# Routing over 1024 tokens at a time, with the router as stationary operand in four column tiles

## What is computed

```python
x = x + 0.5 * ffn(layernorm(x))
x = x + attn(layernorm(x))
x = x + 0.5 * ffn(layernorm(x))

def ffn(x):                       # T = 8192 tokens, E = 32 experts, C = 320
    logits = xt @ w_router        # 512 x 32
    probs = softmax(logits);  top1 = argmax(probs);  gate = probs[top1]
    pos = cumsum(onehot(top1), axis=0)[t, top1] - 1
    accepted = pos < C
    slot = where(accepted, top1 * C + pos, E * C)
    buf[slot] = xt                # gather by expert
    y = (silu(buf @ w_gate) * (buf @ w_up)) @ w_down
    return xt + where(accepted, y[slot] * gate, 0)
```

## Time and profile before

| | us |
|---|---|
| median of 3 runs | 4491.49 (4490.32 to 4492.13) |
| profiled execution, time | 4491.09 |
| profiled execution, span | 4489.0 |
| r1, from the trace | 0 to 218 |
| r2, from the trace | 3414 to 3732 |
| PE busy over the span | 4281.2 (95%) |
| DVE busy over the span | 3158.3 (70%) |

### The profile page before, as it was taken

The page is one execution under the profiler, slowest core; times in us unless marked ns, Lnnn a source line. Parts: engine busy times, 40 slices in busy tenths (PEclk is TensorE's granted clock), DMA queues, the critical chain, the costliest instruction groups (busy, mean ns, idle before and its releaser), DMA issues. The chain is left out here.

```text
span 4489.0 us, 70758 instructions
## 1 busy us (share of the span) xinstructions
PE 4281.2 (95%) x24512; PEld 3068.9 (68%) x24512; DVE 3158.3 (70%) x5967; ACT 2154.7 (48%) x3603; POOL 2726.9 (61%) x1628
## 2 busy tenths in 40 slices
PE   7799999989999989999999999999996997999999
PEld 7789999968888744444444444444444886999998
DVE  7767777756666567777777777777763886777776
ACT  5543333322222136666666666666662443333332
POOL 2333444425555559999999999999992223443343
PEclk9999999989999979999999999999997997999999
DMA  5455555535555534444444444444424765555553
GB/s 181 134 205 187 181 186 187 187 132 176 175 178 178 160 86 96 96 96 96 96 98 99 99 99 99 96 96 97 98 66 166 243 209 183 188 187 183 181 178 117
DMA packets 473572, 650.63 MB, mean 145 GB/s; under 512 B 214300, under 2 KB 216624, under 8 KB 473248
## 3 DMA queue, kind: packets, MB, share of 16 engines
q1 hardware_dynamic: 440480, 579.32, 44.3%
q0 software_dynamic: 30720, 66.62, 3.9%
q10 hardware_dynamic: 2048, 0.53, 0.1%
HBM read 468.75 MB, written 194.58 MB: 148 GB/s over the span
## 5 line engine op out<-in xcount | busy, mean ns | idle before, releaser
L1628 DVE TENSOR_REDUCE att_halves<-att_mx 128x1 f32<-128x512 f32 x2048 | 1274.0, 683 | 487.2 <-PE att_mx L1677 487.1
L1561 ACT ACTIVATE att_p<-att_st 128x512 f32<-128x512 f32 x2048 | 1107.8, 598 | 419.9 <-PE att_st L1693 370.5
L1513 POOL TENSOR_TENSOR att_pairsum<-att_p,att_p 128x1024 f32<-128x1024 f32 x512 | 1209.4, 2386 | 143.3 <-ACT att_p L1561 140.2
L1693 PE MATMUL att_st<-att_q,att_k 128*128 128x512 f32 x2048 | 870.2, 427 | 9.2 <-ACT att_p L1561 4.4
L1677 PE MATMUL att_mx<-att_k,att_q 96*128 96x512 f32 x2048 | 822.1, 406 | 27.0 <-POOL att_q L1502 27.0
L1693 PEld LDWEIGHTS att_st<-att_q,att_k 128*128 128x128 f32 x2048 | 386.2, 189 | 541.0 <-ACT att_p L1561 277.4
L1703 PE MATMUL att_op<-att_p,att_v 128*32 128x512 f32 x4096 | 553.2, 601 | 0.7 <-ACT att_p L1561 0.7
L800 DVE TENSOR_TENSOR e_w<-e_raw,e_w 128x2048 fp32r<-128x2048 f32 x192 | 438.9, 2286 | 42.2 <-ACT e_w L795 42.2
L1677 PEld LDWEIGHTS att_mx<-att_k,att_q 96*128 96x128 f32 x2048 | 394.3, 193 | 108.4 <-issue 27.8
L819 ACT ACTIVATE e_sg<-e_gp 128x320 f32<-128x320 f32 x256 | 112.1, 438 | 731.3 <-PE e_up L182 731.3
L795 ACT ACTIVATE e_w<-e_raw 128x2048 fp32r<-128x2048 f32 x192 | 367.1, 1912 | 42.9 <-DMA e_raw<-in_w_gate 37.6
(11 more groups left out here) (153 smaller groups left out, 8318.5 us busy)
## 6 DMA issues: line engine op xcount, KB each, us to landing
e_raw<-in_w_gate SPq DMA_DIRECT2D x64, 1024.0 KB, 8.7
e_raw<-in_w_up SPq DMA_DIRECT2D x64, 1024.0 KB, 11.0
e_raw<-in_w_down SPq DMA_DIRECT2D x64, 1024.0 KB
att_q<-q SPq DMA_DIRECT2D x192, 256.0 KB, 4.1
att_k<-k SPq DMA_DIRECT2D x192, 256.0 KB, 6.3
r_ao<-ao SPq DMA_DIRECT2D x32, 1024.0 KB, 10.0
r_x<-in_x SPq DMA_DIRECT2D x16, 1024.0 KB, 8.2
x<-r_base SPq DMA_DIRECT2D x16, 1024.0 KB, 5.5
```

The costliest lines, as they stand in the source:

```text
L1513: nc.gpsimd.tensor_tensor(out=pairsum[h][PLACE[g]][:, :], in0=pr[h][2 * g % RING][:, :], in1=pr[h][(2 * g + 1) % RING][:, :], op=ALU.add). ...
L1561: nc.scalar.activation(pr[h][kt % RING][:, half(c)], st[(4 * kt + x) % NB][:, :], ACT.Exp, scale=SCALE).then_inc(s_exp, 1)
L1628: nc.vector.tensor_reduce(out=halves[:, h, qt, c:c + 1], in_=mx[n % NB][:, :], axis=AX.X, op=ALU.max).then_inc(s_max, 1)
L1693: nc.tensor.matmul(st[(4 * kt + x) % NB][:, :], kst[b][:, h, kt * P:(kt + 1) * P], qst[b][:, h, c * HALF:(c + 1) * HALF], start=True, stop ...
```

## The change

- One pass of choice, gates, positions and slots serves two groups, 1024 tokens in 8 tiles (`TR`), with w = r // 2. The tiles of the small quantities are twice as wide.
- `products(r)` now takes a whole group. The router's 128 x 32 slice is the stationary operand, put in column tile j for token tile j, and 128 tokens are streamed: 16 matmuls of 128 columns. The result is transposed, 4 x 32 experts in partitions, and lands in a `tp` tile. ACT copies it (`copy_turned`), and PE turns it back to tokens in partitions (`back`, one transpose of 128 x 128). `xnT` has 2 x 4 buffers, one for each tile of two groups.
- `positions(w)`: one triangular matmul over all 256 columns; for each of the tiles 0 to 6 one matmul of ones with its one-hot repeated over all later tiles (224 to 32 columns); one of ones with the running count repeated 8 times. 9 matmuls instead of 28 per 1024 tokens.
- POOL scatters 8 tiles behind each pass. x has 6 buffers in r1 and 5 in r2.
- The orders of ACT, DVE and PE are written anew, as the diff shows.

```diff
+TR = 2 * TJ
+NR = NG // 2
...
-    NX = 4
+    NX = 5 if attn else 6
...
-        xnT = S.pair(sb, "xnT", [P, KD, P])
+        xnT = [[sb(f"xnT{b}_{j}", [P, KD, P]) for j in range(TJ)] for b in range(2)]
+        turned = S.pair(sb, "turned", [P, P])
...
             def copies(r, js):
                 for j in js:
-                    n = TJ * r + j
-                    act.wait_ge(s_tp, n + 1)
-                    act.wait_ge(s_logits, past(n - 1))
-                    nc.scalar.activation(xnT[j % 2][:, :, :], tp[j % 2][:, :, :], ACT.Copy).then_inc(s_xnT, 1)
-
-            def exps(r):
-                act.wait_ge(s_shifted, r + 1)
-                act.wait_ge(pick.sem, pick.steps * r)
+                    u = (TJ + 1) * r + j
+                    act.wait_ge(s_tp, u + 1)
+                    act.wait_ge(s_logits, past(r - 1))
+                    nc.scalar.activation(xnT[r % 2][j][:, :, :], tp[u % 2][:, :, :], ACT.Copy).then_inc(s_xnT, 1)
+
+            def copy_turned(r):
+                u = (TJ + 1) * r + TJ
+                act.wait_ge(s_tp, u + 1)
+                act.wait_ge(s_logits, past(r - 1))
+                nc.scalar.activation(turned[r % 2][:, :], tp[u % 2][:, 0, :], ACT.Copy).then_inc(s_xnT, 1)
+
+            def exps(w):
+                act.wait_ge(s_shifted, w + 1)
+                act.wait_ge(pick.sem, pick.steps * w)
                 nc.scalar.activation(ex[:, :, :], shifted[:, :, :], ACT.Exp).then_inc(s_exp, 1)
 
...
             norm(0)
             norm(1)
             copies(0, range(TJ))
-            bases(0, range(TJ))
-            for r in range(NG):
-                exps(r)
-                if r + 1 < NG:
-                    copies(r + 1, (0, 1))
-                    bases(r + 1, (0, 1))
-                if r + 2 < NG and not attn:
-                    norm(r + 2)
-                if r + 1 < NG:
-                    copies(r + 1, (2, 3))
-                    bases(r + 1, (2, 3))
-                if r + 2 < NG and attn:
-                    norm(r + 2)
+            if attn:
+                bases(0, range(TJ))
+                for r in range(NG):
+                    copy_turned(r)
+                    if r + 1 < NG:
+                        copies(r + 1, (0, 1))
+                        bases(r + 1, (0, 1))
+                    if r % 2 == 1:
+                        exps(r // 2)
+                    if r + 1 < NG:
+                        copies(r + 1, (2, 3))
+                        bases(r + 1, (2, 3))
+                    if r + 2 < NG:
+                        norm(r + 2)
+            else:
+                norm(2)
+                copy_turned(0)
+                bases(0, range(TJ))
+                copies(1, range(TJ))
+                copy_turned(1)
+                bases(1, range(TJ))
+                for w in range(NR):
+                    r = 2 * w + 2
+                    if r < NG:
+                        copies(r, range(TJ))
+                    exps(w)
+                    if r < NG:
+                        copy_turned(r)
+                        norm(r + 1)
+                        bases(r, range(TJ))
+                        copies(r + 1, range(TJ))
+                        copy_turned(r + 1)
+                    if r + 2 < NG:
+                        norm(r + 2)
+                    if r < NG:
+                        bases(r + 1, range(TJ))
 
...
-            for r in range(NG):
-                if attn and r + 1 < NG:
-                    normalise(r + 1)
-                choose(r)
-                if attn:
-                    gates(r)
-                    if r + 2 < NG:
-                        bias(r + 2)
-                        measure(r + 2, (0, 1))
-                    slots(r)
-                    if r + 2 < NG:
-                        measure(r + 2, (2, 3))
-                else:
-                    if r + 2 < NG:
-                        measure(r + 2, (0, 1))
-                    gates(r)
-                    if r + 2 < NG:
-                        measure(r + 2, (2, 3))
-                    slots(r)
-                    if r + 2 < NG:
-                        normalise(r + 2)
+            if attn:
+                for r in range(NG):
+                    w = r // 2
+                    if r + 1 < NG:
+                        normalise(r + 1)
+                    if r % 2 == 0:
+                        if r + 2 < NG:
+                            bias(r + 2)
+                            measure(r + 2, (0, 1))
+                        if r + 3 < NG:
+                            bias(r + 3)
+                        if r + 2 < NG:
+                            measure(r + 2, (2, 3))
+                    else:
+                        if r + 2 < NG:
+                            measure(r + 2, (0,))
+                        choose(w)
+                        if r + 2 < NG:
+                            measure(r + 2, (1,))
+                        gates(w)
+                        if r + 2 < NG:
+                            measure(r + 2, (2,))
+                        slots(w)
+                        if r + 2 < NG:
+                            measure(r + 2, (3,))
+            else:
+                measure(2, range(TJ))
+                normalise(2)
+                for w in range(NR):
+                    r = 2 * w + 3
+                    choose(w)
+                    if r < NG:
+                        measure(r, range(TJ))
+                    gates(w)
+                    if r < NG:
+                        normalise(r)
+                    if r + 1 < NG:
+                        measure(r + 1, range(TJ))
+                    slots(w)
+                    if r + 1 < NG:
+                        normalise(r + 1)
 
...
             def turn(r, j):
-                n = TJ * r + j
-                pe.wait_ge(s_xn, n + 1)
-                pe.wait_ge(s_xnT, past(n - 1))
+                u = (TJ + 1) * r + j
+                pe.wait_ge(s_xn, TJ * r + j + 1)
+                pe.wait_ge(s_xnT, past(u - 1))
                 for k in range(KD):
-                    last = nc.tensor.transpose(tp[j % 2][:, k, :], xn[r % 2][:, j, k * P:(k + 1) * P], ident[:, :])
+                    last = nc.tensor.transpose(tp[u % 2][:, k, :], xn[r % 2][:, j, k * P:(k + 1) * P], ident[:, :])
                 last.then_inc(s_tp, 1)
 
-            def products(r, j):
-                pe.wait_ge(s_xnT, TJ * r + j + 1)
-                pe.wait_ge(s_shifted, r)
-                pe.wait_ge(s_top, 2 * TJ * r)
+            def products(r):
+
+                u = (TJ + 1) * r + TJ
+                pe.wait_ge(s_xnT, u)
                 for k in range(KD):
-                    last = nc.tensor.matmul(logits[:, j, :], xnT[j % 2][:, k, :], wr_sb[:, k, :],
-                                            start=k == 0, stop=k == KD - 1)
-                last.then_inc(s_logits, 1)
-
-            def positions(r):
+                    for j in range(TJ):
+                        last = nc.tensor.matmul(tp[u % 2][j * E:(j + 1) * E, 0, :], wr_sb[:, k, :], xnT[r % 2][j][:, k, :],
+                                                start=k == 0, stop=k == KD - 1)
+                last.then_inc(s_tp, 1)
+
+            def back(r):
+                w, par = r // 2, r % 2
+                pe.wait_ge(s_xnT, (TJ + 1) * (r + 1))
+                pe.wait_ge(s_shifted, w)
+                pe.wait_ge(s_top, 2 * TR * w)
+                nc.tensor.transpose(logits[:, par * TJ:(par + 1) * TJ, :].rearrange("p j e -> p (j e)"),
+                                    turned[par][:, :], ident[:, :]).then_inc(s_logits, 1)
+
+            def positions(w):
 
                 pe.wait_ge(s_setup, 1)
-                pe.wait_ge(s_onehot, r + 1)
-                pe.wait_ge(s_run, r)
-                pe.wait_ge(s_slots, r)
-                for j in range(TJ):
-                    nc.tensor.matmul(posp[:, j, :], tri[:, :], onehot[:, j, :], start=True, stop=False)
-                    for before in range(j):
-                        nc.tensor.matmul(posp[:, j, :], ones[:, :], onehot[:, before, :], start=False, stop=False)
-                    last = nc.tensor.matmul(posp[:, j, :], ones[:, :], run[:, :], start=False, stop=True)
-                last.then_inc(s_pos, 1)
+                pe.wait_ge(s_onehot, w + 1)
+                pe.wait_ge(s_run, w)
+                pe.wait_ge(s_slots, w)
+                nc.tensor.matmul(posp[:, :, :], tri[:, :], onehot[:, :, :], start=True, stop=False)
+                for j in range(TR - 1):
+                    nc.tensor.matmul(posp[:, j + 1:TR, :], ones[:, :],
+                                     onehot[:, j:j + 1, :].broadcast_to([P, TR - 1 - j, E]), start=False, stop=False)
+                nc.tensor.matmul(posp[:, :, :], ones[:, :], run[:, :].unsqueeze(1).broadcast_to([P, TR, E]),
+                                 start=False, stop=True).then_inc(s_pos, 1)
 
             if attn:
                 for r in range(2):
                         project(r, j)
             pe.wait_ge(s_const, 16 * n_const)
```

(91 more changed lines are left out.)

69 lines of the change are left out of this document (33 added, 36 removed).

## The result

The changed kernel takes 4431.73 us (median of 4 runs, 4431.13 to 4435.49) against 4491.81 (4490.32 to 4492.66) for the kernel before beside it: a ratio of 0.9868, 95% interval 0.9851 to 0.9885. The forecast was 4450, the range 4431 to 4478: right in sign and in the mechanism that it named, 18 us short in size, and 0.7 us inside the lower edge of the range. The profiled execution is 4431.1 us with a span of 4429.3, to be set against 4491.1 and 4489.0.

A forecast was written before the change was run, and what follows sets the result against it. Routing 1 was taken as bound by a closed PE-DVE loop, routing 2 by PE and DVE both full. Routing 1 -19.4, routing 2 -24.6, missed loads +3 gave -41 from 4491.1: 4450 us, range 4431 to 4478.

The forecast's parts named there:

- first MAX8: Start of the first pair's choice on DVE: forecast at 33.7 us in routing 1 and at 3480 in routing 2.
- 16.7 + 2P: Routing 1's loop per pair, with P the products' time: 20.9 us, 2.8 less than now.
- P: Time of a group's column-tile products on PE: 2.1 us at 1.2 GHz, 1.1 at 2.4.
- rival C: Routing 1: new stream takes PE to 2.4 GHz, loop is DVE's 18.3 us; 4429 us in all, chance 0.11.
- Last interval: Routing 1's last interval between pairs, which lacks a normalisation: 19.0 us.
- tail: End of routing 2, from the last pair's choice to the last scatter: 18.3 us.
- 29.9 + P: Routing 2's loop per pair, with P the products' time: 31.0 us, against 34.3.
- The last term: Routing 2: 3 us added over the stage for attention-output loads that miss, 13.0 us being left for 12.6.
- Rival D: Routing 2: attention output lands 2 us late, pair 33 us, 12 us go back; 4462 us, chance 0.13.
- the chain: Routing 1's loop: choice, positions, products, copied logits, table load, root, then bases, copies, turns, products, normalise; 20.9 us per pair.
- B: Both routings: weight loads not hidden under the column tiles, P 3.5 and 1.9; 4476 us, chance 0.14.
- E: Both routings: column tiles run one after the other, P 7 and 3.8; slower, 4549 us, chance 0.04.

The follow-up runs named there:

- root_first: Changed kernel with, in ACT's order in routing 1, a group's square root ahead of the copy of the logits in front of it: 4427.5 us.
- prod_twice: Changed kernel with each group's products summed twice over, 64 matmuls in place of 32: 4501.8 us.
- x_four: Changed kernel with four x buffers in both routings in place of six and five: 4462.0 us.
- x_four_shifted: Changed kernel with four x buffers and, in routing 1, 64 unused matmuls of 32 columns ahead of PE's first turn: 4434.0 us.
- wide_only: Changed kernel with the old products, tokens as weight and nothing turned back; choice, positions and slots still over 1024 tokens: 4484.1 us.
- old_positions: Changed kernel with the positions as before, 44 matmuls of 32 columns in place of 9: 4471.9 us.
- old_positions_root: Changed kernel with the positions' 44 small matmuls and, in routing 1, the root ahead of the copied logits: 4461.2 us.
- back_early: Changed kernel with routing 2's two transposes back ahead of the next projection on PE: 4427.6 us.
- both_orders: Changed kernel with routing 1's root ahead of the copied logits and routing 2's transposes back ahead of the projection: 4420.9 us.
- filler: Changed kernel with unused matmuls of 512 columns in routing 1, 8 behind each even group's products and 4 behind the transposes back: 4429.7 us.
- tiles_only: Kernel before with only the column-tile products turned back; choice, positions and slots stay over 512 tokens: 4553.1 us.
- tiles_tuned: Kernel before with column-tile products over 512 tokens, the changed kernel's orders and, in routing 1, the root ahead of the copied logits: 4471.9 us.

## Why the prediction was right, and where its sizes were off

- Routing 1, first MAX8: 32.04 for 33.7. 1.7 us less.
- Routing 1, six intervals: 116.7 us for 125.4. Forecast 16.7 + 2P with P 2.1. P was 1.94 at 1.2 GHz and the pair there 20.0 to 20.2, 2.4 us less over three pairs: 0.3 a pair is P, the rest the 0.42 us that I put twice between products and copy, where the rows have 0.06 (133.43 + 1.94 to 135.43). The other 6.3 us are the level: it did not stay, and three pairs of the high level or partly so had 18.4 to 19.6. This is rival C, half true: I gave it 0.11 because no stretch of the earlier trace rows showed the high level. 8.7 us, the largest miss.
- Last interval: 15.0 for 19.0, 4.0 us. The interval also lacks four measurements of 0.8 us on DVE, which I left out, but they were not on its path: DVE stood 2.23 us for the logits. It is the level again. Two sets of products at 1.08 for 2.1 give 2.0 us, positions 0.5 (0.71 for 1.25), the second group's turns and copies 0.4, the results between products and copy 0.7. Both sets of products here had rival C's level.
- From the last MAX8 to the last scatter: 18.7 for 18.3.
- Routing 2: first MAX8 63.7 us after the stage's start (65.5 forecast), six intervals 186.2 (185.7), last 21.0 (21.4), tail 18.2 (18.3). The form 29.9 + P held at three values of P: 1.08 (30.8), 1.96 (32.0), 3.65 (33.6 to 34.6). The last term, 3 us for loads that miss, was nothing: from 3500 to 3640 they landed in at most 11.1 us, and once the stage had its first data PE never waited for DMA. Rival D falls; 4.7 us over the stage.
- Sum: 1.7 + 8.7 + 4.0 - 0.3 + 4.7 = 18.8 us, which is what lies between forecast and run. Some 10 of them are PE's level in routing 1 (6.3 in the pairs, up to 4 in the last interval). The time is nearer to rival C's 4429 than to 4450, and that it lies in the range at all, by 0.7 us, owes something to luck: the range's edge stood at C. What the runs do bear out is the chain: where PE is at 1.2 GHz the pair follows it, and with the root taken out of it (root_first) every pair is DVE's 18.4.
- Rivals B and E fall by P 1.94 and 1.08 (B asked for 3.5 and 1.9). The Trainium skill ("TensorE: Matmul & The Clock Gate", Part 3, the list in The mechanism) would have weights overlap running matmuls only in another row group; the trace does not agree: 32 weights of one row group left 1.08 us for four steps of 128 columns in four tiles, where the stream alone was put at 0.98 to 0.99, and a second set of 32 added 0.88 (prod_twice).

One thing the forecast's method could not see. It took the loop's waits for the whole of its length. x_four and x_four_shifted show that the same work in the same order can take 28 us more or less by something that stands in no engine's work. The 60 us between the two kernels hold for the programs as they are laid out; the 33.5 of routing 1 may hold some us of that either way.

## What to carry to other kernels

Where two engines are both full, price their reliefs together: in routing 2, 12.7 and -1.0 us alone became 25.9. Where a result goes PE, ACT, PE, DVE, keep the next group's small but urgent step (here the root) from queueing behind its copy; moving that one instruction made routing 1's loop independent of PE's clock. In a stage of short instructions under full DMA traffic, time a kernel with a few unused instructions ahead before believing a difference of tens of microseconds.

## What the runs showed of the hardware

- 64 unused matmuls of 32 columns at the start of a stage took 24.4 us off it (211.1 to 186.7; 28.0 off the kernel); four x buffers for six, with no wait for x, had added 26.5 to it. Why is open.
- The 32 product records in four column tiles take 1.08 us at 2.4 GHz and 1.94 at 1.2, a second set behind them 0.88 and 1.7 more; the same products with the tokens as stationary operand take 3.65 us at 2.4 GHz (wide_only).
- Between 50 and 150 us DVE waits for its own results, up to 1.6 us at a time (for the copy of the indices up to 2.5, put down to "remote"), in prod_twice, wide_only, old_positions, old_positions_root and x_four, and routing 1 ends at 211 to 244. It never does in the changed kernel, root_first, back_early, both_orders, filler and x_four_shifted, and routing 1 ends at 180 to 189. The three kernels with passes of 512 tokens (before, tiles_only, tiles_tuned) have one such wait of 0.5 us each and end at 212 to 222.
- The granted clock in the profile's rows and the durations can disagree: over 40 to 160 us the kernel before has 1.00 with turns as long as at 1.2 GHz, the changed kernel's pair from 128.65 0.50 with the same durations. The length of a known matmul is the safer witness.
- 12 matmuls of 512 columns a pair that compute nothing took the turns of routing 1 to 2.4 GHz (granted clock 0.91 from 40 to 160 us, 0.63 without them).
